# Two graph layers on one core: six of eight banks of the last two attention rows transposed by DMA, and the first and last row blocks reordered

## The reference

```python
# x: 4096 x 128 f32, adj: 4096 x 4096 f32 of zeros and ones (about one in 1024 is set)
deg = clip(adj.sum(axis=1), 1.0); dis = deg ** -0.5
diffusion = (dis[:, None] * adj * dis[None, :]) @ x - x
sim = x @ x.T / (norms[:, None] * norms[None, :])
attn = softmax(beta * sim * adj, axis=1)
x = layernorm(x + diffusion + sigmoid(alpha) * (attn @ x - x))
x = layernorm(x + relu(adj @ (x @ weights)))
```

## Time and profile before

| | before |
|---|---|
| median of the runs | 658.79 us |
| lowest, highest | 658.75, 659.19 us |
| the profiled execution, own time | 658.59 us |
| its span, first to last instruction | 656.7 us |
| TensorE busy | 638.0 us (97%) |
| VectorE busy | 517.8 us (79%) |
| ScalarE busy | 412.2 us (63%) |
| GpSimd busy | 236.8 us (36%) |
| chain that ended last, by engine | PE 86%, DVE 4%, DMA 4%, ACT 2% |

### The profile page before, as it was taken

One profiled execution on the slowest core, in us unless ns is written; L12 is line 12 of the kernel. 1 busy time (PEld: TensorE's weight loads), 2 busy tenths in 40 slices (PEclk: granted clock), 3 DMA queues, 4 the chain that ended last, 5 costly groups with the idle time before them and its releaser, 6 DMA issues.

```text
span 656.7 us, 16155 instructions
## 1 busy us (share of the span) xinstructions
PE 638.0 (97%) x5087; PEld 463.5 (71%) x5087; DVE 517.8 (79%) x1565; ACT 412.2 (63%) x768; POOL 236.8 (36%) x249
## 2 busy tenths in 40 slices
PE   7788999999999999999999999999999999999996
PEld 6456777777777777777777777888888864444465
DVE  4987999999999999999999998878777773334443
ACT  6998999999999999999999998612111110000000
POOL 5998553553554554544544546400000000000000
PEclk9999999999999999999999999999999999999999
DMA  7878999999999999999999996300000000000000
GB/s 282 303 161 215 278 272 239 279 256 253 280 267 239 285 263 233 285 263 242 292 258 240 307 237 97 77 1 1 0 0 0 0 0 1 16 17 16 16 33 33
DMA packets 165019, 107.36 MB, mean 163 GB/s; under 512 B 144384, under 2 KB 148608, under 8 KB 164992
## 3 DMA queue, kind: packets, MB, share of 16 engines
q1 hardware_dynamic: 164992, 107.04, 61.6%
HBM read 69.27 MB, written 2.10 MB: 109 GB/s over the span
## 4 chain that ended last, share of the span: by engine, by line
PE 86%; DVE 4%; DMA 4%; ACT 2%; issue 2%; POOL 1%; DVEq 0%; SPq 0%; POOLq 0%; ACTq 0%
PE ps_s L1005 22%; PE ps_s L1198 17%; PE ps_e L1170 15%; PE ps_e L1016 8%; PE ps_e L1038 8%; PE ps_acc L1038 7%; PE ps_e L1041 4%; PE ps_acc L1041 4%; DMA eTx<-e_parts 2%; DVE scores L708 1%; DMA x_keep<-in_x 1%; PE ps_e L1054 1%; DVE e_parts L729 1%; PE ps_acc L1182 1%; PE ps_s L1054 1%
## 5 line engine op out<-in xcount | busy, mean ns | idle before, releaser
L1005 PE MATMUL ps_s<-xn_parts,xn_signed 128*128 128x512 f16 x756 | 203.3, 379 | 4.2 <-DVE cmax L708 4.2
L708 DVE CUSTOM_DVE_ANT_1 scores<-ps_s,adj_bytes 128x512 f32<-128x512 f32 x252 | 171.6, 683 | 24.4 <-PE ps_s L1005 15.2
L523 ACT ACTIVATE scores<-scores,col 128x1024 f32<-128x1024 f32 x128 | 157.4, 1232 | 2.1 <-DVE col L719 1.9
L482 ACT ACTIVATE adj_bytes<-land 128x1024 uint8<-128x1024 f32 x128 | 133.5, 1047 | 0.6 <-POOL packed L343 0.6
L351 POOL TENSOR_SCALAR e_parts<-scores 128x1024 f16<-128x1024 f32 x64 | 68.5, 1071 | 157.7 <-ACT scores L523 154.2
L1170 PE MATMUL ps_e<-y_parts,stage 128*128 128x256 f16 x896 | 98.0, 273 | 0.0
L1005 PEld LDWEIGHTS ps_s<-xn_parts,xn_signed 128*128 128x128 f16 x756 | 68.4, 98 | 40.2 <-DVE cmax L708 4.3
L1170 PEld LDWEIGHTS ps_e<-y_parts,stage 128*128 128x128 fp8e4 x896 | 87.7, 98 | 10.1
L530 ACT ACTIVATE eT_parts<-ps_e 128x512 f16<-128x512 f32 x128 | 75.8, 595 | 28.7 <-PE ps_e L1016 27.9
L723 DVE SCALAR_TENSOR_TENSOR eT_parts<-ps_e,eT_parts 128x512 f16<-128x512 f32 x128 | 87.4, 683 | 1.9 <-ACT eT_parts L530 1.9
L729 DVE SCALAR_TENSOR_TENSOR e_parts<-scores,e_parts 128x1024 f16<-128x1024 f32 x64 | 88.4, 1382 | 0.4 <-POOL e_parts L351 0.4
(11 more groups left out here) (128 smaller groups left out, 967.1 us busy)
## 6 DMA issues: line engine op xcount, KB each, us to landing
land<-in_adj SPq DMA_DIRECT2D x128, 512.0 KB, 5.4
x_keep<-in_x SPq DMA_DIRECT2D x4, 512.0 KB, 5.6
out<-u SPq DMA_DIRECT2D x7, 256.0 KB, 2.1
eTx<-e_parts SPq DMA_TRANSPOSE x64, 4.3
packT<-packed SPq DMA_TRANSPOSE x16, 6.5
out<-u SPq DMA_DIRECT2D x2, 128.0 KB, 1.7
scores<-in_L_gnn_weights SPq DMA_DIRECT2D x1, 64.0 KB, 2.0
col<-in_L_gnn_beta SPq DMA_DIRECT2D x1, 0.5 KB, 7.1
```

The costliest lines, as they stand in the source:

```text
L482: nc.scalar.activation(adj_bytes[:, q, i * CH:(i + 1) * CH], land[:, q, i, :], ACT.Copy, scale=float(BYTE_TOP[q] >> i), accum_out=deg[:, i ...
L523: nc.scalar.activation(piece, piece, ACT.Exp, bias=neg_max[q], scale=abs_beta, accum_out=csum[:, q, i:i + 1]).then_inc(exp_done, 1)
L708: nc.vector.tensor_tensor_reduce(scores[:, q, o:o + BANK].rearrange("p (k q) -> p k q", k=K), score_bank(h, r == 0 if start else False).re ...
L1005: ins = nc.tensor.matmul(score_bank(h, start), xn_signed[:, q, part, :], xn_parts[:, other, o:o + BANK], start=(part == 0 and other == 0), ...
```

## The change

In the last two row blocks (30 and 31) piece 1 of E (banks 2 and 3) is no longer transposed on TensorE. GpSimd writes its high part (`third_high`) and VectorE its low part (`third_low`) into a part of the first half of `land`, which is free by then, and SP transposes it by DMA (`turn_third`) into another part of it. The transposes, e_highs and e_lows of banks 2 and 3 of these rows are gone; banks 0 and 1 use PSUM banks of their own (`ps_e[:, b]`). The orders of all engines for these two rows are rewritten; both use `LATE_ATTEND`, now (0, 1, 4, 5, 6, 7, 2, 3). In GpSimd's order `third_high(0)` stands ahead of the last `pack` and `y_rows(2)` ahead of the two last `ex_high`.

In the first rows TensorE's order of cosines, transposes and attends is rewritten, VectorE's too (`x_low(1)` moves from before `e_low(0, 0)` to behind `e_low(0, 3)`), ScalarE does `exps(1, 1, 2)` before `cast(2, 0, 1)` and `norm_root(1)` before `squares(2)`, and SP issues two pieces of row block 4's adjacency ahead of `turn_adj(0, 0)` and of `turn_ex(1, 1, 1)`.

```diff
-    LATE_ATTEND = (0, 4, 5, 1, 6, 7, 2, 3)
+    LATE_ATTEND = (0, 1, 4, 5, 6, 7, 2, 3)
...
+        spare = land[:, 0, :, :].rearrange("p i j -> p (i j)").bitcast(F16)
+        third = spare[:, 0:2 * CH].rearrange("p (a j) -> p a j", a=2)
+        thirdT = [spare[:, (1 + m) * 2 * CH:(2 + m) * 2 * CH].rearrange("p (t i) -> p t i", i=P) for m in range(2)]
# SP
+            def row_4(i):
+                sp.wait_ge(cast_done, 2 * C + i + 1)
+                land_piece(1, 0, i)
+            row_4(0)
+            row_4(1)
             turn_adj(0, 0)
+            turn_ex(1, 1, 1)
+            row_4(2)
+            row_4(3)
+            turn_ex(2, 0, 0)
...
-            for r in range(R - G + 1, R):
-                turn_ex(r, r % 2, 1)
-                if r < R - 1:
-                    turn_ex(r + 1, (r + 1) % 2, 0)
+            def turn_third(m):
+                sp.wait_ge(third_lo, m + 1)
+                sp.dma_start_transpose(thirdT[m], third.rearrange("p a j -> p (a j)")).wait_op(
+                    x_loaded[0], 16, "sem-ge").then_inc(third_turned, 16)
+            turn_ex(R - 3, 1, 1)
+            turn_ex(R - 2, 0, 0)
+            turn_ex(R - 2, 0, 1)
+            turn_third(0)
             turn_adj(R // 2 - 1, 1)
-            sp.wait_ge(e_turned, R * TB)
+            turn_ex(R - 1, 1, 0)
+            turn_ex(R - 1, 1, 1)
+            turn_third(1)
+            sp.wait_ge(e_turned, R * TB - TB)
# GpSimd
+            def third_high(m):
+                pool.wait_ge(exp_done, (R - 2 + m) * C + C)
+                if m == 0:
+                    pool.wait_ge(cast_done, (R - 1) * C)
+                else:
+                    pool.wait_ge(third_turned, 16)
+                nc.gpsimd.tensor_scalar(third[:, 0, :], scores[:, m, CH:2 * CH], E_SCALE, 1.0,
+                                        ALU.mult, ALU.mult).wait_op(sign_done, 1, "sem-ge").then_inc(third_hi, 1)
...
             ex_high(R - 2, 0, 1)
+            third_high(0)
             pack(R - 1, 1, R // 2 - 1, 1)
...
             y_rows(1)
+            y_rows(2)
             ex_high(R - 1, 1, 0, place=1)
             ex_high(R - 1, 1, 1, place=1)
-            y_rows(2)
+            third_high(1)
             y_rows(3)
# ScalarE, last rows
-            e_high(R - 2, 0)
-            e_high(R - 2, 1)
+            late_e_high(0, 0)
+            late_e_high(0, 1)
...
-            e_high(R - 2, 2)
             exps(R - 1, 1, 0, LAST_EXP)
+            exps(R - 1, 1, 2, LAST_EXP)
             y_high(0)
-            e_high(R - 2, 3)
-            exps(R - 1, 1, 2, LAST_EXP)
             exps(R - 1, 1, 3, LAST_EXP)
-            e_high(R - 1, 0, order=LATE_ATTEND)
-            e_high(R - 1, 1, order=LATE_ATTEND)
+            late_e_high(1, 0, LATE_ATTEND)
+            late_e_high(1, 1, LATE_ATTEND)
+            exps(R - 1, 1, 1, LAST_EXP)
             y_high(1)
-            exps(R - 1, 1, 1, LAST_EXP)
-            e_high(R - 1, 2, order=LATE_ATTEND)
-            e_high(R - 1, 3, order=LATE_ATTEND)
# VectorE, first rows
-            mask(1, 1, 0, start=True)
-            mask(1, 1, 1, start=True)
-            x_low(1)
+            for h in range(4):
+                mask(1, 1, h, start=True)
             e_low(0, 0)
-            mask(1, 1, 2, start=True)
-            mask(1, 1, 3, start=True)
+            mask(1, 1, 4, start=True)
             e_low(0, 1)
             ex_low(0, 0, 0)
-            mask(1, 1, 4, start=True)
             mask(1, 1, 5, start=True)
             ex_low(0, 0, 1)
-            e_low(0, 2)
             mask(1, 1, 6, start=True)
             mask(1, 1, 7, start=True)
             row_max(1, 1)
+            e_low(0, 2)
+            mask(2, 0, 0)
             e_low(0, 3)
-            mask(2, 0, 0)
+            x_low(1)
             mask(2, 0, 1)
# VectorE, last rows
-            e_low(R - 2, 1)
+            late_e_low(0, 1)
+            third_low(0)
...
-            e_low(R - 2, 2)
-            y_low(0)
-            e_low(R - 2, 3)
             attn_add(R - 3, 1)
             total_step(R - 2, 0, 2)
-            e_low(R - 1, 0)
+            y_low(0)
             ex_low(R - 1, 1, 0)
-            e_low(R - 1, 1)
+            late_e_low(1, 0)
+            late_e_low(1, 1)
+            ex_low(R - 1, 1, 1)
             y_low(1)
-            ex_low(R - 1, 1, 1)
-            e_low(R - 1, 2)
-            e_low(R - 1, 3)
+            third_low(1)
             attn_add(R - 2, 0)
# TensorE, first rows
             cosines(1, 1, 1)
+            cosines(1, 1, 2)
             turn_e(0, 0, 0, True, FIRST_EXP)
             turn_e(0, 0, 1, True, FIRST_EXP)
-            cosines(1, 1, 2)
             cosines(1, 1, 3)
             cosines(1, 1, 4)
+            cosines(1, 1, 5)
             first_attend(0)
-            cosines(1, 1, 5)
+            cosines(1, 1, 6)
             first_attend(1)
             turn_e(0, 0, 2, True, FIRST_EXP)
             turn_e(0, 0, 3, True, FIRST_EXP)
-            cosines(1, 1, 6)
             cosines(1, 1, 7)
+            cosines(2, 0, 0)
+            cosines(2, 0, 1)
             first_attend(2)
-            cosines(2, 0, 0)
             first_attend(3)
-            cosines(2, 0, 1)
+            cosines(2, 0, 2)
             first_attend(4)
-            cosines(2, 0, 2)
             cosines(2, 0, 3)
# TensorE, last rows
-            late_attend(0)
-            turn_e(R - 2, 0, 2)
-            late_attend(1)
-            late_attend(2)
-            late_attend(3)
-            turn_e(R - 2, 0, 3)
-            late_attend(4)
...
-            late_attend(7)
+            for k in range(H):
+                attend(R - 2, 0, k, order=LATE_ATTEND, late=True)
...
-            turn_e(R - 1, 1, 0, order=LAST_EXP)
-            turn_e(R - 1, 1, 1, order=LAST_EXP)
+            late_turn_e(1, 0, LAST_EXP)
+            late_turn_e(1, 1, LAST_EXP)
             first_sums(0)
             last_attend(0)
             last_attend(1)
-            turn_e(R - 1, 1, 2, order=LAST_EXP)
-            turn_e(R - 1, 1, 3, order=LAST_EXP)
             first_sums(1)
-            for k in range(2, H):
+            for k in range(2, 6):
                 last_attend(k)
             first_sums(2)
+            last_attend(6)
+            last_attend(7)
             first_sums(3)
```

More of the change, by code:

```diff
@@ L280, in turn @@
                 turn_ex(r + 1, 1 - q, 0)
-            for k in range(G):
+            for k in range(1, G):
                 turn(1, k)
@@ L495, in _ @@
             norm_root(0)
+            norm_root(1)
             squares(2)
-            norm_root(1)
             block_squares(3, 0)
@@ L852, in _, with late_e_low, third_low @@
                 row(R - 14 + n, n % 2, spread=(n // C, n % C))
+            def late_e_low(m, b):
+                dve.wait_ge(e_hi, (R - 2) * TB + (2 * m + b + 1))
+                nc.vector.scalar_tensor_tensor(eT_parts[:, b, 1, :], ps_e[:, b, :], E_SCALE,
+                                               eT_parts[:, b, 0, :], ALU.mult, ALU.subtract).then_inc(e_lo, 1)
+            def third_low(m):
+                dve.wait_ge(third_hi, m + 1)
+                nc.vector.scalar_tensor_tensor(third[:, 1, :], scores[:, m, CH:2 * CH], E_SCALE,
+                                               third[:, 0, :], ALU.mult, ALU.subtract).then_inc(third_lo, 1)
             mask(R - 1, 1, 4)
-            e_low(R - 2, 0)
+            late_e_low(0, 0)
             ex_low(R - 2, 0, 1)
@@ L1018, in turn_e, with attend @@
                 ins.then_inc(e_turned, 1)
-            def attend(r, q, k, start=False, early=False, order=ATTEND_ORDER):
+            def attend(r, q, k, start=False, early=False, order=ATTEND_ORDER, late=False):
                 b = order[k]
-                if b < TB:
+                if late and b < 2:
+                    pe.wait_ge(e_lo, (R - 2) * TB + (2 * q + b + 1))
+                elif late and b < TB:
+                    pe.wait_ge(third_turned, 16 * q + 16)
+                elif b < TB:
                     pe.wait_ge(e_lo, r * TB + (b + 1))
@@ L1033, in attend @@
                     t, slot = TH * b + SLOT[n], TH * (b % 2) + n
-                    if b < TB:
+                    if b < (2 if late else TB):
                         hi, lo = (eT_parts[:, b, a, n * P:(n + 1) * P] for a in range(2))
+                    elif b >= TB:
+                        hi, lo = (eTx[:, q, b // 2 - 2, a * TC + slot, :] for a in range(2))
                     else:
-                        hi, lo = (eTx[:, q, b // 2 - 2, a * TC + slot, :] for a in range(2))
+                        hi, lo = (thirdT[q][:, a * TC + slot, :] for a in range(2))
                     nc.tensor.matmul(attn_ps[q][:, 0:2 * D], hi, x_parts[:, t, :],
@@ L1118, in _, with late_turn_e @@
                 row(r + 1, 1)
-            turn_e(R - 2, 0, 0)
+            def late_turn_e(m, b, order=EXP_ORDER):
+                if b == 0:
+                    pe.wait_ge(exp_done, (R - 2 + m) * C + (order.index(0) + 1))
+                pe.wait_ge(e_lo, (R - 2) * TB + (0 if m == 0 else b + 1))
```

(24 more changed lines are left out.)

9 lines of the change are left out of this document (8 added, 1 removed).

## The result

The changed kernel takes 666.19 us (median of 4 runs, 664.59 to 668.21) beside 658.88 us (4 runs, 658.75 to 659.19) for the kernel before: ratio 1.0108, 95% interval 1.0084 to 1.0131. A second series gave 666.57 us (6 runs) beside 659.1 us (15 runs): 1.0110, 1.0088 to 1.0131. So it is 7.3 to 7.5 us slower, where I forecast 2.2. The direction was right; the time lies 3 us outside my range. The runs of the changed kernel spread over 3.6 us in the first series and 4.3 in the second, and the profiled one (668.21 us, span 666.0) is the slowest of its four, 2.0 above their median.

What follows compares the result with a forecast made beforehand. TensorE, busy 97%, bounds the kernel, with GpSimd full in the first rows. 658.59 us + 1.1 (first rows) + 1.1 (last rows) = 660.8, and 0.2 to the median: 661.0 us, range 657.4 to 663.2.

Steps and rivals of the forecast that it cites:

- The clock: Rival, 12%: TensorE's long idle stretches each bring the lower clock, 2.2 us each, 0.9 covered on the first; 664.5 us.
- The stall on `x_low`: First rows: TensorE idles from 37.3 to 41.3 awaiting `x_low(1)`, starts row block 1 at 44.6; the 3.2 us are covered.
- The gate at full clock: First rows: VectorE's mask, awaiting all `minus_x` and releasing TensorE's cosine, comes 1.1 us later (range 0 to 2.4).
- The squares at nothing: First rows: reordered squares cost nothing, as `norm_root(1)` fills ScalarE's wait for x; under 1 us if uncovered.
- Last rows' waits: Last two rows: 21.9 us of work plus 5.4 us idle makes 27.3 against 26.2, so +1.1 us.
- (a): Last rows: TensorE waits 1.5 us for `e_low` before row 30's second attend, now bank 1.
- (b): Last rows: TensorE waits 2.8 us for row 30's third half row, transposed by DMA and landing at 414.1.
- (c): Last rows: TensorE waits 1.0 to 1.1 us for `y_low(1)`, done at 421.2.
- (d): Last rows: the second third half row lands at about 428.8, wanted at 429.2; no wait, 0.4 us to spare.
- Landings, casts, masks at nothing: First rows: reordered casts and landings cost nothing, under 1 us if uncovered; masks ahead of `x_low` carry it to about 39.

Runs made afterwards that it cites:

- f1: The changed kernel with 14 identity matmuls filling the stall ahead of the third first attend: 664.18 us, ratio 1.0077.
- f3: The kernel before with the last rows' change alone, 6 and 8 identity matmuls put into waits (a) and (b): 661.01 us, ratio 1.0027.
- f2: The changed kernel with `x_low(1)` ahead of `e_low(0, 0)` and `squares(2)` ahead of `norm_root(1)`, both as before: 662.25 us, ratio 1.0044.
- e5: The kernel before with only `x_low(1)` moved behind `e_low(0, 3)`: 661.38 us, ratio 1.0033.
- e0: The changed kernel run again, unaltered: 666.57 us, ratio 1.0110.
- e2: The kernel before with only the five reordered places in the first rows: 664.39 us, ratio 1.0074.
- e4: The changed kernel with `squares(2)` put back ahead of `norm_root(1)`: 665.58 us, ratio 1.0093.
- e8: The changed kernel with 32 identity matmuls ahead of the third first attend and 14 in place of 3 in the opening: 669.48 us, ratio 1.0161.
- e7: The changed kernel with 32 identity matmuls ahead of the third first attend: 669.68 us, ratio 1.0158.
- g3: The changed kernel with `x_low(1)` and `squares(2)` at their old places and the last rows' waits filled with 6 and 8 identity matmuls: 661.13 us, ratio 1.0033.
- e1: The change with its five reordered places in the first rows put back, so the last rows' change alone: 662.16 us, ratio 1.0034.

## Why the prediction was wrong

- **The clock**: the step that failed, and the largest. The sum has no term for it; it was a rival with 12%, and it happened. Behind the stall it costs 2.0 to 2.5 us in the median (f1), in the last rows 0.5 to 0.8 (f3; 1.2 to 1.6 in the executions in which it falls), and in the opening, which the rival lacked, perhaps 1.0 to 1.6 (f2). The rival's 2.2 us behind the stall were the right size, but it took 0.9 of them off as cover, and that cover wasn't there. I kept its chance low because no row of before had an idle stretch of over 1.4 us in a running kernel. But the opening's 4.3 us at half rate were such a row, and the Trainium skill, TensorE: Matmul & The Clock Gate, Part 1, has idleness as the cause, which I quoted beside it. A rival that both a row and a page speak for should have had half the chance at least.
- **The stall on `x_low`**: right, and at full clock to 0.2 us (f1: attend at 41.14, row block 1 at 44.41), in a profile whose opening kept its clock.
- **The gate at full clock**: mis-sized, +2.1 us in f1 where the sum has 1.1. The 1.1 was `x_low`'s hold on GpSimd alone. GpSimd's chain also waits for what follows from row block 1's cosines on TensorE: ScalarE's exponentials (2.79 us in the changed kernel and in e5) and the transposed half row (1.73 us in the changed kernel, 2.33 in f1). The half row was named in the prediction, for the upper end of the range of this term, 2.4 us, and left out of the sum; f1's 2.1 is that case. TensorE's own late start was covered in f1, with 1.12 us of idle time left at the gate, but the gate moves with it: from the start of row block 1 to the gate it was 17.96 us before and 16.3 to 17.4 in the profiles with a late TensorE (changed 16.39, e0 16.38, e2 16.40, e4 16.38, e5 16.27, f1 17.06, e8 17.17, e7 17.41), so only 0.5 to 1.7 us of a late start did not reach it.
- **The squares at nothing**: probably wrong. I priced their cover on ScalarE, "under 1 us", and not what the moved idle time ahead of the transposes does to TensorE's clock; the 1.0 to 1.6 us rest on pairs whose intervals overlap.
- **Last rows' waits**: right as a sum: 27.35 us to the end of the sums where I had 27.3. Of its parts (a) was 1.9 for 1.5, (b) 2.2 for 2.8, (c) 0.7 for 1.1 and (d) nothing; the profile counts each about 0.2 us shorter than the step between the matmuls around it, which makes 5.4 of the 4.9.
- **Landings, casts, masks at nothing**: right while `x_low` is early (g3 beside f3). With `x_low` late, SyncE's two landings stand in the chain that sets the gate (f1), and what they cost there was not measured.

The account of the 7.3 to 7.5 us: 1.1 the waits of the last rows, 0.5 to 0.8 the clock there, 2.1 the late gate at full clock, 2.0 to 2.5 the clock behind the stall, 1.0 to 1.6 the clock in the opening. The terms were measured in different pairs and overlap: f1 still has some of the opening's. The sum is 6.7 to 8.1. What shows the causes together is g3: with `x_low` and the squares back and the last waits filled, 2.0 us are left of the 7.3 to 7.5. One thing stays open: f3 loses 1.8 us in the median and only 1.1 of it is in the stretch. Ahead of row block 30 the profiles differ by a wait of 0 to 1.05 us for a DMA transpose at 77 to 84 us (none before, 0.42 in f3, 0.68 in e1, 1.05 in e5), in kernels whose code there is the same; whether the last rows' change makes it longer on average wasn't tested.

## What to carry to other kernels

Before an idle stretch is taken as cover, follow what ends it back to its origin: if the chain behind the late engine runs through that same engine, the slack is only the part that is another engine's own. The chain can run through a DMA queue too: a reordering that costs nothing while everything is on time can stand in the way when something is late. An idle stretch on TensorE of 3 to 4 us is paid twice where it ends in a low clock, so price the clock with every stall that an edit makes, the opening's too. And when taking work off a busy engine by giving some to two that exclude each other, count their turns first: here 1.75 us taken off TensorE came back as waits in four orders out of four.

## What the runs showed that I had not expected

- All five unfilled idle stretches of 3.4 to 4.3 us in the first rows (the two profiles of the changed kernel, e2, e4, e5) were followed by matmuls at half rate; filled with idle work that ends before the awaited instruction (f1) the clock stayed at 1.00. Shorter ones went both ways: in the last rows a pair of about 1.9 and 2.2 us (3.0 in e8) was followed by a lower clock in five profiles of nine.
- The scatter of the times goes with the clock: of e0's six runs the fastest (663.43 us) has a granted clock of 0.996, the slowest (667.76) 0.988. All six of g3 have 0.999 or more and lie within 1.3 us. The kernel before, at 0.995 to 1.000, lies within 3.2 us over 18 runs, so not all scatter is the clock's.
- VectorE's instructions of 1.22 us with two SBUF inputs took up to 2.91 us beside GpSimd's 1.9 us multiplications, more than the 1.58 that I had read ahead.
- A 128-column fp32 identity matmul is two records of 0.11 to 0.12 us each: 64 records in 7.31 us for 32 instructions (e8), 28 in 3.29 for 14 (f1).
